# A transformer block's attention: the rows of score maxima turned by VectorE and DRAM instead of TensorE

## The reference

```python
ada = jax.nn.silu(c) @ W_ada + b_ada
shift_msa, scale_msa, gate_msa, shift_mlp, scale_mlp, gate_mlp = jnp.split(ada, 6, axis=-1)
h = _modulate(_layernorm(x), shift_msa, scale_msa)
x = x + gate_msa * _attention(h, W_qkv, b_qkv, W_proj, b_proj)
h = _modulate(_layernorm(x), shift_mlp, scale_mlp)
mlp = jax.nn.gelu(h @ W_fc1 + b_fc1, approximate=True) @ W_fc2 + b_fc2
return x + gate_mlp * mlp
```

## Time and profile before

| | |
|---|---|
| median of 3 runs | 3295.42 us (3295.06 to 3297.61) |
| the profiled execution | 3297.75 us, its span 3296.0 us |
| granted TensorE clock | 0.999 of full |
| TensorE matmuls busy | 3279.6 us |
| VectorE / ScalarE / GpSimd busy | 2147.5 / 1695.9 / 359.6 us |
| attention, first to last matmul | 415.1 to 2220.1 us |

### The profile page before, as it was taken

The page is one execution under the profiler, slowest core; times in us unless marked ns, Lnnn a source line. Parts: engine busy times, 40 slices in busy tenths (PEclk is TensorE's granted clock), DMA queues, the critical chain, the costliest instruction groups (busy, mean ns, idle before and its releaser), DMA issues. The chain is left out here.

```text
span 3296.0 us, 52551 instructions
## 1 busy us (share of the span) xinstructions
PE 3279.6 (100%) x19303; PEld 2147.2 (65%) x19303; DVE 2147.5 (65%) x4008; ACT 1695.9 (51%) x3183; POOL 359.6 (11%) x284
## 2 busy tenths in 40 slices
PE   9999999999999999999999999999999999999999
PEld 7888744444444444444444444449988898989888
DVE  6445478888888888888888888857543433433332
ACT  4323367777777777777777777765511111211110
POOL 0000010111100000010000000026411010000000
PEclk9999999999999999999999999999999999999999
DMA  7554442333323231323232232318632122421211
GB/s 238 177 164 145 145 98 53 72 72 66 71 47 74 43 79 43 81 44 75 48 67 56 59 63 50 72 49 276 221 108 83 45 72 85 134 74 53 83 45 54
DMA packets 145167, 295.35 MB, mean 90 GB/s; under 512 B 22079, under 2 KB 45119, under 8 KB 137998
## 3 DMA queue, kind: packets, MB, share of 16 engines
q1 hardware_dynamic: 144910, 291.99, 33.1%
HBM read 192.95 MB, written 97.26 MB: 88 GB/s over the span
## 5 line engine op out<-in xcount | busy, mean ns | idle before, releaser
L1307 DVE TENSOR_REDUCE q_mx<-b_st 128x1 f32<-128x512 f32 x1512 | 990.1, 682 | 231.7 <-PE b_st L1235 227.9
L1383 ACT ACTIVATE b_pt<-b_st 128x512 f32<-128x512 f32 x2048 | 1055.7, 611 | 9.5 <-PE b_st L1255 9.5
L1267 PE MATMUL b_op<-b_pt,b_vs 128*37 128x512 f32 x4096 | 1008.5, 601 | 2.1 <-DVE b_ob L1350 2.1
L1376 ACT ACTIVATE b_early<-b_st 128x512 f32<-128x512 f32 x504 | 301.2, 598 | 479.0 <-PE b_st L1235 477.1
L1267 PEld LDWEIGHTS b_op<-b_pt,b_vs 128*37 128x37 f32 x4096 | 215.3, 113 | 367.8 <-issue 263.6
L1307 DVE TENSOR_REDUCE q_mx<-b_early 128x1 f32<-128x512 f32 x504 | 339.8, 674 | 0.0
L2128 PE MATMUL d_pm<-d_vh,d_ah 128*128 128x288 f32 x1152 | 339.3, 295 | 0.4 <-DVE d_al L2166 0.4
L2129 PE MATMUL d_pm<-d_vl,d_ah 128*128 128x288 f32 x1152 | 339.4, 295 | 0.0
L2130 PE MATMUL d_pm<-d_vh,d_al 128*128 128x288 f32 x1152 | 339.3, 295 | 0.0
L1447 POOL TENSOR_TENSOR w_oc<-b_oa,b_ob 37x512 f32<-37x512 f32 x127 | 161.2, 1270 | 1468.5 <-DVE b_ob L1350 1464.3
L1235 PEld LDWEIGHTS b_st<-q_hh,b_qa 36*128 36x128 f32 x1024 | 129.9, 184 | 222.8 <-DVE q_mx L1307 145.2
(11 more groups left out here) (412 smaller groups left out, 4770.0 us busy)
## 6 DMA issues: line engine op xcount, KB each, us to landing
qkh<-a_th SPq DMA_DIRECT2D x72, 256.0 KB, 2.1
qkl<-a_tl SPq DMA_DIRECT2D x72, 256.0 KB, 2.4
d_yi<-y SPq DMA_DIRECT2D x64, 288.0 KB, 3.0
n_oi<-hw SPq DMA_DIRECT2D x12, 1024.0 KB, 5.7
vd<-a_vx SPq DMA_DIRECT2D x8, 1184.0 KB, 6.8
b_vs<-vd SPq DMA_DIRECT2D x32, 296.0 KB, 7.5
a_x<-in_x SPq DMA_DIRECT2D x8, 1152.0 KB, 6.7
q_qs<-qkh SPq DMA_DIRECT2D x32, 288.0 KB
```

Of the source, the lines that this page charges most:

```text
L1267: ins = e.matmul(op[64 * a:64 * a + VW, :], vs[h % 2][:, j + 8 * a, :], pt[g % NP][:, a * 512:a * 512 + 512], start=j == 0, stop=j == 7)
L1307: e.tensor_reduce(mx[:, k // 2, col:col + 1], src, AX.X, ALU.max).then_inc(s_mx, 1)
L1376: e.activation(early[:, :], bank(slot)[:, :], ACT.Copy).then_inc(s_cp, 1)
L1383: e.activation(pt[g % NP][:, a * 512:a * 512 + 512], bank(k)[:, :], ACT.Exp, scale=SCALE).then_inc(s_p, 1)
```

## The change

It has four parts. (1) The column is turned by VectorE: `nm` becomes [128, 32], a 32x32-block transpose gives `nt`, from which `mh` and `ml` [128, 32] come; all four instructions stand together in `row_max`, right behind the group's last unit. (2) SyncE writes `mh` and `ml` to a DRAM tensor `md`, waits for both, and reads four rows of `qb` back from it, 16 pieces of 128 bytes each. TensorE's matmul and the ring's use for it are gone. (3) A head's load is in two parts: `qa`/`ka` at hb % 16 == 0, `qb`/`kb` at hb % 16 == 8, with a semaphore each. (4) The 16 units in QKV all lie in chunk 7, two a step in v0 to qk3, the second one in the banks `pt`; the turning of group 0 goes to qk4 to qk7 and stays on TensorE.

```diff
+    md = dram("md", [2, 128, 32])
...
     def maxima(c, kind, n):
-        k = (NF + 4) * (c - HCH - 2) + (n + 4 if kind == "qk" else n)
-        return range(k, k + 1) if 0 <= k < 2 * UQ else range(0)
+        k = 2 * (n + 4 if kind == "qk" else n)
+        return range(k, k + 2) if c == NCH - 1 and k < 2 * UQ else range(0)
...
-                if n:
-                    e.wait_ge(s_mx, 2 * n - 1 + a)
-                e.matmul(sp[a][:, :], qs0[r, queries], ks0[r, keys], ...)
+                if n > 1:
+                    e.wait_ge(s_mx, 2 * n - 3 + a)
+                e.matmul((pt if n % 2 else sp)[a][:, :], qs0[r, queries], ks0[r, keys], ...)
...
-        s.slot = None if s.late is None else use("mh", s.late)
...
         def max_rows(p):                     # SyncE
             for j, m in enumerate((mh, ml)):
                 e.wait_ge(s_mh, 2 * p - 1 + j)
+                e.dma_start(md[j, :, :], m[:, :].bitcast(F)).then_inc(s_md, 16)
+            e.wait_ge(s_md, 32 * p)
+            for j in range(2):
                 for r in (ROWS - 2 + j, 64 + ROWS - 2 + j):
-                    e.dma_start(qb[...][r:r + 1, u * 512:u * 512 + 512].bitcast(F), m[:, :].bitcast(F))
+                    e.dma_start(qb[...][r:r + 1, u * 512:u * 512 + 512].bitcast(F),
+                                md[j, :, :].rearrange("(b c) t -> c b t", b=4)[0:4, :, :])
...
                 if r == 0 and h + 1 < NH:
-                    load(h + 1)
+                    load(h + 1, rows_a, qa, ka, s_qa)
+                if r == 8 and h + 1 < NH:
+                    load(h + 1, rows_b, qb, kb, s_qb)
...
-        def max_rows(p, slot):               # TensorE
-            e.wait_ge(s_nm, p + 2)
-            bank_free(e, slot)
-            e.matmul(bank(slot)[0:VW, 0:128], nm[p % 2][:, :], ident[:, :], start=True, stop=True).then_inc(s_mt, 1)
...
         def row_max(p):                      # VectorE
+            e.wait_ge(s_nm, p)
+            if p > 1:
+                e.wait_ge(s_mx, 2 * (UQ * (p + 1) - THERE))
+                e.wait_ge(s_mt, p - 1)
+            q = p % 4 * 4
+            e.tensor_reduce(nm[:, 0:4], mx[:, q:q + 4, :], AX.X, ALU.max, negate=True).then_inc(s_nm, 1)
             e.wait_ge(s_nm, p + 1)
...
+            e.transpose(nt[:, :], nm[:, :]).then_inc(s_mt, 1)
             e.wait_ge(s_mt, p)
             rows_there(e, p - 1)
-            src = bank(slot)[0:4, 0:128]
-            e.tensor_copy(mh[:, :], src).then_inc(s_mh, 1)
+            e.tensor_copy(mh[:, :], nt[:, :]).then_inc(s_mh, 1)
             e.wait_ge(s_mh, 2 * p - 1)
-            e.tensor_tensor(ml[:, :], src, mh[:, :].bitcast(F), ALU.subtract).then_inc(s_mh, 1)
+            e.tensor_tensor(ml[:, :], nt[:, :], mh[:, :].bitcast(F), ALU.subtract).then_inc(s_mh, 1)
```

More of the change, by code:

```diff
@@ L396, in program @@
                     with ExitStack() as ctx:
-                        rest = phase_attention(nc, Scope(nc, ctx, "b", top), W, tile, ident, qs0, ks0, qb0, k1, mx, mh, ml,
-                                                gd, W_proj, b_proj, xf, qkh, qkl, vd, ot, sm)
+                        rest = phase_attention(nc, Scope(nc, ctx, "b", top), W, tile, ident, qs0, ks0, qb0, k1, mx,
+                                               gd, md, W_proj, b_proj, xf, qkh, qkl, vd, ot, sm)
                     N = Ahead(Scope(nc, late, "n", top, "right"), [hh0, ah0], [lo0, al0],
@@ L406, in program, with phase_qkv @@
                               b_fc2)
-def phase_qkv(nc, A, ident, adaT, eps, bq, sc, qs0, ks0, qb0, hh0, lo0, mx, nm, mh, ml, gd, xf, cond, W_ada,
+def phase_qkv(nc, A, ident, adaT, eps, bq, sc, qs0, ks0, qb0, hh0, lo0, mx, gd, xf, cond, W_ada,
               b_ada, W_qkv, b_qkv, qkh, qkl, vd):
@@ L433, in phase_qkv @@
     row0 = A.sb("row0", [66, 640])
+    nm, mh, ml = A.sb("nm", [128, 4]), A.sb("mh", [4, 128], R), A.sb("ml", [4, 128], R)
     wa = A.sb("wa", [128, KT, C])
@@ L621, in sync @@
                         modulation(vi, p)
-                    if (c, n) == (NCH - 1, 1):
+                    if (c, n) == (NCH - 1, 7):
                         max_rows()
@@ L697, in score_max @@
                 e.wait_ge(s_q0, 128)
+                e.wait_ge(s_hf, KT * NCH)
             queries, keys = slice(qb * 128, qb * 128 + 128), slice(k * 512, k * 512 + 512)
@@ L700, in score_max @@
                 r = slice(64 * a, 64 * a + D)
-                if n:
-                    e.wait_ge(s_mx, 2 * n - 1 + a)
-                e.matmul(sp[a][:, :], qs0[r, queries], ks0[r, keys], start=True, stop=True).then_inc(s_s, 1)
+                if n > 1:
+                    e.wait_ge(s_mx, 2 * n - 3 + a)
+                e.matmul((pt if n % 2 else sp)[a][:, :], qs0[r, queries], ks0[r, keys], start=True, stop=True).then_inc(s_s, 1)
         def max_rows():
@@ L795, in tensor @@
                     score_max(m)
-                if (c, kind, n) == (NCH - 1, "v", 3):
+                if (c, kind, n) == (NCH - 1, "qk", 5):
                     max_rows()
@@ L913, in vector @@
                         k4 = m % 2 * 2 + a
-                        e.tensor_reduce(mx[:, m // 2, k4:k4 + 1], sp[a][:, :], AX.X, ALU.max).then_inc(s_mx, 1)
-                if (c, kind, n) == (NCH - 1, "v", 2):
+                        e.tensor_reduce(mx[:, m // 2, k4:k4 + 1], (pt if m % 2 else sp)[a][:, :], AX.X, ALU.max).then_inc(
+                            s_mx, 1)
+                if (c, kind, n) == (NCH - 1, "qk", 4):
                     e.wait_ge(s_mx, 4 * UQ)
                     e.tensor_reduce(nm[:, :], mx[:, 0:4, :], AX.X, ALU.max, negate=True).then_inc(s_nm, 1)
-                elif (c, kind, n) == (NCH - 1, "qk", 0):
+                elif (c, kind, n) == (NCH - 1, "qk", 6):
                     e.wait_ge(s_mt, 1)
@@ L1056, in phase_attention @@
     ob = [A.sb(f"ob{i}", [VW, 512]) for i in range(2)]
-    nm = [A.sb(f"nm{i}", [128, VW]) for i in range(2)]
+    nm, nt = A.sb("nm", [128, 32]), A.sb("nt", [128, 32])
+    mh, ml = A.sb("mh", [128, 32], R), A.sb("ml", [128, 32], R)
     qa, qb = [qs0, A.sb("qa1", [128, L], R)], [qb0, A.sb("qb1", [128, L], R)]
@@ L1066, in phase_attention @@
     ring += [A.ps(f"st{i}", [128, 512]) for i in range(3, 7)]
-    s_qk, s_m, s_v, s_o = A.sems("qk", NB), A.sems("m", NB), A.sems("v", 2), W.s_o
+    (s_qa, s_qb), s_m, s_v, s_o = A.sems("qk", 2), A.sems("m", NB), A.sems("v", 2), W.s_o
     s_one = A.sem("one")
     s_s, s_mx, s_nm, s_mt, s_mh = A.sem("s"), A.sem("mx"), A.sem("nm"), A.sem("mt"), A.sem("mh")
-    s_cp = A.sem("cp")
+    s_cp, s_md = A.sem("cp"), A.sem("md")
     s_st, s_p, s_pv, s_oa, s_oc = A.sem("st"), A.sem("p"), A.sem("pv"), A.sem("oa"), A.sem("oc")
@@ L1120, in bank_free, with loaded @@
                 e.wait_ge(s_mx, n if n % 4 == 1 else n + 1)
-            elif kind == "mh":
-                e.wait_ge(s_mh, 2 * n)
             else:
                 e.wait_ge(W.s_u, n + 1)
-    def loaded(e, h):
+    def loaded(e, h, sem):
         if h:
-            e.wait_ge(s_qk[h % NB], 256 * (h // NB + h % NB))
+            e.wait_ge(sem, 128 * h)
     def rows_there(e, p):
@@ L1144, in sync, with load @@
     def sync(e):
-        def load(h):
+        def load(h, rows, q, k, sem):
             i, b, hd = h % NB, h // H, h % H
@@ L1152, in load @@
                 tile.stored(e)
-            for rows, q, k in ((rows_a, qa[i], ka[i]), (rows_b, qb[i], kb[i])):
-                for dst, r, src, f0, n, t, w in rows(q, k, qkh, qkl, hd * D, C + hd * D, b * L):
-                    e.dma_start(dst[r:r + n, :].bitcast(F), src[f0:f0 + n, t:t + w]).then_inc(s_qk[i], 16)
+            loaded(e, h - 1, sem)
+            for dst, r, src, f0, n, t, w in rows(q[i], k[i], qkh, qkl, hd * D, C + hd * D, b * L):
+                e.dma_start(dst[r:r + n, :].bitcast(F), src[f0:f0 + n, t:t + w]).then_inc(sem, 16)
         def load_v(h):
@@ L1208, in sync @@
                 W.load_x(e, 0, W.x1, xf)
+        e.wait_ge(s_qa, 128 * (NH - 1))
+        e.wait_ge(s_qb, 128 * (NH - 1))
         for i in range(NB):
-            e.wait_ge(s_qk[i], 256 * (NH // NB - 1 + i))
             e.wait_ge(s_m[i], 64 * (4 * NH // NB - 1 + i))
@@ L1230, in score_max @@
             if k == 0:
-                loaded(e, h)
+                loaded(e, h, s_qa)
             for a in range(2):
@@ L1246, in scores_t @@
             if j == 0:
+                loaded(e, h, s_qb)
                 rows_there(e, p)
@@ L1285, in tensor @@
                 products(2 * s.now)
-            if s.late is not None:
-                max_rows(s.late, s.slot)
             if s.now is not None:
@@ L1296, in score_max @@
             if p > 4:
-                e.wait_ge(s_nm, p - 2)
+                e.wait_ge(s_nm, p - 3)
             m, c = 2 * (n - THERE), k % 2
@@ L1309, in row_max @@
         def row_max(p):
+            e.wait_ge(s_nm, p)
[4 more added lines that the diff above has]
+            e.tensor_reduce(nm[:, 0:4], mx[:, q:q + 4, :], AX.X, ALU.max, negate=True).then_inc(s_nm, 1)
             e.wait_ge(s_nm, p + 1)
```

(10 more changed lines are left out.)

11 lines of the change are left out of this document (4 added, 7 removed).

## The result

3257.34 us (median of 4, 3255.73 to 3259.51) against 3296.52 us before on the same chip (median of 4); ratio 0.9877, 95% interval 0.9865 to 0.989.

A forecast was written before the change was run, and what follows sets the result against it. TensorE was taken to bound attention, its steps lengthening with its work. -26.3 us there and -2.6 in QKV, all else 0, made -28.9: 3268.9 from the profiled execution, 3266.5 from the runs' median; range 3263 to 3282.

The forecast's parts named there:

- the sum itself: Whole kernel: -26.3 in attention and -2.6 in QKV make -28.9 us, from 3297.75 to 3268.9, or x 0.9912.
- The turning: Attention's 127 late steps: without TensorE's turning matmul each gets 0.207 us shorter, -26.3 us in all.
- VectorE's part: Attention: four small VectorE instructions, 0.72 to 1.01 us a group, cost 0, covered by 2.2 us of rest in four steps.
- The way through DRAM: Attention, each group's rows written and read back by SyncE: 7.5 us of 13.4 available, so 0 at the likeliest.
- the landing of writes: Hand-over of a group's rows: the wait until the writes to md land in DRAM, taken as 2.1 us.
- the reads' issue: SyncE's queue: four reads of a group's rows from md, 0.6 us each, 2.4 us together.
- A late row: Attention's loaded groups: one landing of 7.5 us delays VectorE some 0.5 us a head, 31 heads, +15: 3282; chance 0.12.
- Part 4: QKV's units paired in chunk 7: -3.2 us, less 0.6 of waiting, net -2.6; bounds -3.2 to +0.6.
- The units: QKV: 16 x 0.64 = 10.2 us before, 8 x (0.64 + 0.24) = 7.0 after, so -3.2 us.
- stall: QKV's q/k steps: four VectorE reductions a step hold banks 0.1 to 0.3 us too long in three steps, 0.6 in all.
- the end of QKV: Group 0's late turning: SyncE's four DMAs fit into 2.4 us of free queue before a store, 0, at most 0.3 us.
- The slower rival: Attention: every landing takes 7.5 us, the chain 18.3 against 13.4, 4.9 late once a head, +152: 3418; chance 0.05.

The follow-up runs named there:

- e1_placed: The kernel before with only the tiles nm, mh and ml moved out from among the long-lived tiles: 3288.60 us against 3298.16, ratio 0.9974.
- e11_old_places: The kernel after with QKV's nm, mh and ml back in their old place among the long-lived tiles: 3267.30 us against 3298.30, ratio 0.9906.
- e10_full_line: The kernel after with an unused tile of 64 bytes where nm, mh and ml stood: 3261.14 us, ratio 0.9887.
- e6_load_whole: The kernel after with each head's 16 loads again in one go at hb % 16 == 0: 3316.27 us, ratio 1.0057.

## Why the prediction was wrong, point by point

- **The step that failed** is the sum itself: "-26.3 - 2.6 = -28.9 against the profiled execution's own time". It took every matmul that the change doesn't name as unchanged. Moving three small tiles changed where operands lie in SBUF, and QKV, projection and MLP got 9.5 us shorter (`e1_placed`, in the traces; its medians give 9.6, after against `e11_old_places` 10.0). The kernel's diff has it, in the lines that move `nm`, `mh` and `ml` to another scope; the prediction says nothing of them, and its range's lower end, 3263, had no term for it. With QKV's tiles put back, `e11_old_places` has the 0.9906 that the prediction has as 0.9912.
- **The turning, -26.3**: right. 0.207 us a late step was measured by doubling as 0.202 by the runs and 0.220 by the steps, and late steps are now like the others. Attention as a whole gained 28.6 us in `e11_old_places`, 2.3 more. Some 1.2 of it are few ns in each step: ordinary ones went from 3.459 to 3.457 us in the mean, late ones from 3.669 to 3.457. The first two steps take 9.3 for 9.7 us. No run takes the few ns apart, but places alone can do as much: an ordinary step is 3.456 us in `e1_placed`, and 3.455 in `e10_full_line`.
- **VectorE's part, 0**: right. The four small ones take 0.77 us busy and 0.9 us from start to end, where 0.72 to 1.01 was estimated.
- **The way through DRAM, 0**: right with the load split; the landing of writes was over-sized (1.5 for 2.1 us), the reads' issue a little under-sized (0.63 for 0.6). The reasoning that the whole load would reach into the next group and that part 3 cuts that is what `e6_load_whole` shows. A late row was priced at 0.5 us a head; there VectorE waits 1.7 us for it in the mean, and each of the 31 heads costs 1.9 us; the fallen clock comes on top of the waits, and the prediction had no term for it.
- **Part 4, -2.6**: right in sum, 2.6 by the trace and 2.9 by the runs, and partly by luck. The units gave the 3.2 us (the second one of a pair costs 0.23 where 0.24 was taken), no stall took 0.6 of it away, and the end of QKV cost 0.6 us that the prediction has as "0, at most 0.3".
- **The slower rival** (every hop late) did not come about; the same mechanism with another load schedule does exist and costs 59 us.

## What to carry to other kernels

When a kernel's bound engine has no gaps, the price of an instruction is what the repeating step grows by, and doubling it on the chip gives the same number. A hand-over through DRAM costs nothing as long as the DMAs ahead of it in the queues are short against its slack, so the size of the pieces that other loads come in belongs to the same change. And a diff that moves, adds or drops a tile moves all tiles behind it: compare the pitch of untouched matmuls before crediting the difference to the edit, and keep some tenths of a per cent in the range for it.

## What the runs showed of the hardware

- 512-column matmuls with 128 rows and columns, at full clock, started every 227 to 235 ns depending on where tiles lie in SBUF: q_hh against a_wh every 227.7 ns in the kernel after, and every 233.1 to 233.6 with a_wh 32, 64 or 1056 bytes higher. Over this kernel it is 9.6 us of 3298, 0.3% (`e1_placed`).
- A VectorE transpose of 128x32 in float32 took 0.21 us.
- Writes of 16 KB to DRAM in 128 pieces of 128 bytes landed in 1.4 to 1.5 us (median of 127), and in up to 8.3 us. The kernel after has 66,783 DMA packets of under 512 bytes where before had 22,079, and no engine in it waited for `md`.
- A DMA that writes one partition's row from several pieces took 0.57 us of SyncE's queue with 4 pieces from SBUF and 0.60 with 16 from DRAM; one of 36 whole rows took 0.36.
- TensorE's granted clock fell from full to half behind 5 of the 30 waits of `e6_load_whole` in attention, four of them of 1.5 to 1.8 us and one of 7.7; a wait of 2.05 us (ended at 1529.41) had no such stretch behind it.
